# A two-layer macaron network in one kernel: norms, recurrence and routing laid between the units of the two expert mixtures

## What is computed

```
x = x + 0.5 * moe(layernorm(x))          # first mixture
x = x + rwkv(layernorm(x))               # recurrence over the tokens
x = x + 0.5 * moe(layernorm(x))          # second mixture, same weights
x = x + 0.5 * quant_ffn(layernorm(x))
x = x + attention(layernorm(x))          # 16 heads, softmax over all 2048 tokens
x = x + 0.5 * quant_ffn(layernorm(x))

moe(x):  logits = x @ router_w + router_b;  the two best of 8 experts, softmax over those two -> gates
         h = relu(x @ w1[e] + b1[e])     # 128 -> 512, for every expert e
         sum over e of gates[:, e] * (h @ w2[e] + b2[e])
rwkv(x): x_prev = x one token earlier;  k, v, r from three mixes of x and x_prev
         p' = max(p + w, k);  a' = exp(p+w-p')*a + exp(k-p')*v;  b' likewise without v
         out = (sigmoid(r) * (e1*a + e2*v)/(e1*b + e2)) @ Wo
layernorm(x) = (x - mean) / sqrt(var + eps), over the 128 channels, no gain and no bias
```

## Time and profile before

| what | value |
|---|---|
| median of 3 runs | 2174.58 us (2172.72 to 2175.76) |
| the profiled execution's own time | 2179.51 us |
| its span, first to last instruction | 2177.7 us |
| TensorE matmul busy | 2010.9 us, 92% |
| VectorE busy | 1852.0 us, 85% |
| ScalarE busy | 1521.1 us, 70% |
| GpSimd busy | 1414.8 us, 65% |
| mean granted TensorE clock | 0.944 |

### The profile page before, as it was taken

How to read it: one execution, slowest core, us unless ns; L and a number is a source line. 1 busy time by engine, 2 the same in 40 slices (tenths; PEclk the granted TensorE clock), 3 DMA queues, 4 the chain that set the end, 5 groups by cost and what they waited for, 6 DMA issues and landing times. The chain is left out here.

```text
span 2177.7 us, 25650 instructions
## 1 busy us (share of the span) xinstructions
PE 2010.9 (92%) x8288; PEld 1438.4 (66%) x8288; DVE 1852.0 (85%) x2001; ACT 1521.1 (70%) x1873; POOL 1414.8 (65%) x660
## 2 busy tenths in 40 slices
PE   5999638999869999999999999999999999999877
PEld 4888427887546766766766676676766667666545
DVE  5888886887677999899899899989989989999885
ACT  4666435665417878788788787877878888788753
POOL 1000010000308999899989989989998998999872
PEclk6999758998779999999999999999999999999987
DMA  2210002110050303123031231312313122130000
GB/s 105 76 49 30 0 0 60 49 49 15 4 116 6 71 15 74 28 55 76 13 74 31 52 67 23 73 20 62 69 21 68 30 58 57 31 69 17 5 1 20
DMA packets 77272, 94.68 MB, mean 43 GB/s; under 512 B 31755, under 2 KB 35211, under 8 KB 76870
## 3 DMA queue, kind: packets, MB, share of 16 engines
q1 hardware_dynamic: 77142, 93.04, 18.8%
HBM read 41.11 MB, written 1.42 MB: 20 GB/s over the span
## 5 line engine op out<-in xcount | busy, mean ns | idle before, releaser
L490 POOL TENSOR_TENSOR p_l<-p_raw,p_h 128x1024 fp32r<-128x1024 f32 x512 | 1241.8, 2457 | 148.1 <-ACT p_h L1068 133.2
L1065 ACT ACTIVATE p_raw<-ps 128x1024 f32<-128x1024 f32 x512 | 567.2, 1108 | 241.7 <-PE ps L711 240.9
L1387 DVE TENSOR_REDUCE m_part<-ps 128x1 f32<-128x1024 f32 x480 | 584.9, 1218 | 125.7 <-PE ps L688 124.7
L1068 ACT ACTIVATE p_h<-ps 128x1024 fp32r<-128x1024 f32 x512 | 523.4, 1022 | 0.0
L710 PE MATMUL ps<-qa,ka 128*128 128x512 f32 x1024 | 445.8, 435 | 2.0 <-ACT m_t L1036 2.0
L711 PE MATMUL ps<-qb,kb 65*128 65x512 f32 x1024 | 409.2, 400 | 0.0
L725 PE MATMUL ps<-p_h,v_hl 128*128 128x512 f32 x1024 | 402.6, 393 | 1.1 <-POOL p_l L490 0.9
L1381 DVE TENSOR_REDUCE l_sum<-p_raw 128x128 f32<-128x1280 f32 x256 | 377.2, 1477 | 0.4
L688 PE MATMUL ps<-ka,qa 128*128 128x512 f32 x960 | 314.9, 409 | 12.6 <-DVE m_part L1387 12.4
L728 PE MATMUL ps<-p_l,v_hl 128*64 128x512 f32 x1024 | 321.3, 395 | 0.0
L1367 DVE TENSOR_REDUCE p_raw<-p_raw 128x128 f32<-128x1024 f32 x256 | 309.2, 1209 | 12.2 <-ACT p_raw L1065 12.2
(11 more groups left out here) (187 smaller groups left out, 2653.4 us busy)
## 6 DMA issues: line engine op xcount, KB each, us to landing
big<-g_scratch SPq DMA_DIRECT2D x64, 256.0 KB, 3.2
xnp<-r_scratch SPq DMA_DIRECT2D x59, 256.0 KB, 3.9
qa<-qk_hi SPq DMA_DIRECT2D x112, 128.0 KB, 2.3
ka<-qk_hi SPq DMA_DIRECT2D x56, 128.0 KB, 2.4
kb<-qk_hi SPq DMA_DIRECT2D x56, 128.0 KB, 2.4
ka<-xnp SPq DMA_DIRECT2D x28, 128.0 KB, 2.4
qb<-xnp SPq DMA_DIRECT2D x28, 128.0 KB, 2.4
ka<-qk_low SPq DMA_DIRECT2D x28, 128.0 KB, 3.7
```

The lines of the kernel that those rows point to most:

```text
L490: nc.gpsimd.tensor_tensor(p_l[:, g % 4, :, :], slots(g), p_h[:, g % 4, :, :].bitcast(fp32), ALU.subtract).then_inc(pl_done, 1)
L1065: af(slots(g), s_t, ACT.Exp).then_inc(raw_done, 1)
L1068: af(p_h[:, g % 4, :, :], s_t, ACT.Exp).then_inc(ph_done, 1)
L1387: nc.vector.tensor_reduce(m_part[:, it, half:half + 1], ps[:, 4:6, :].rearrange("p b n -> p (b n)"), AX.X, ALU.max).then_inc(s_max, 1)
```

## The change

**One loop.** The six steps up to `layer_norm(3)` are replaced by `mixtures()` on each engine: a loop over ticks. In tick t (0 to 255) TensorE makes the first product of unit t and the second product of unit t - 4. Norm, routing, recurrence and weight preparation are cut into chunks of 512 tokens (weights: one expert), and each of their operations has a tick, by constants written by hand. 16 ticks precede the first unit.

**Bias in a weight row.** After a norm the 128 channels of a token sum to zero, so x[127] = -(sum of the others) and x @ w = sum over c < 127 of x[c] * (w[c] - w[127]). Row 127 of x becomes a row of ones, and row 127 of w1 becomes b1. The eviction then needs no bias: ScalarE writes relu straight into `h_h` (fp32r), and VectorE makes the low part from PSUM, max(ps, 0) - h_h. For this SP also loads w1's last row, repeated over 127 partitions, and VectorE subtracts it.

**Other moves.** The low parts of x and of w1 and the adding of an expert to x go from VectorE to GpSimd (0.5 goes into the gates' eviction); the recurrence's products with v, e1 and r are on GpSimd. `layer_norm(3)` waits for all expert additions at once. Layer 1 is the same but for the numbers that it waits for.

The core of the diff:

```diff
+TICKS = 2 * NC * UNITS
+HEAD_START = 16
+ROUTE_AT = (-16, 0, 20, 59, 95, 131, 167, 187)
+RWKV_AT = (40, 76, 112, 148)
+WEIGHTS_AT = (-8, -5, 2, 6, 10, 14, 18, 22)
+WEIGHT_PARTS = ((0, 1), (1, 2), (2, 4), (4, 8))
+N_MEAN, N_CEN, N_SQR, N_VAR, N_STD, N_REC, N_SPREAD, N_OUT = 0, 1, 1, 4, 5, 6, 8, 9
+R_HIGH, R_LOGITS, R_LOW, R_TOP, R_SECOND, R_EXP, R_GATES, R_TURN, R_ROWS = 10, 11, 11, 12, 13, 14, 15, 18, 19
+K_EXP = (18, 19, 20, 21)
+W_BASE, W_HI, W_LO, W2_HI, W2_LO = 0, 1, 1, 2, 3
...
 SP:
-            sp.dma_start(w1_raw, a["w1T"]).then_inc(w1_loaded, 16)
-            sp.dma_start(w2_raw, a["w2T"]).then_inc(w2_loaded, 16)
+            def load_weights(i):
+                lo, hi = WEIGHT_PARTS[i]
+                sp.dma_start(w1_raw[0:C - 1, lo:hi, :], a["w1T"][0:C - 1, lo:hi, :]).then_inc(w1_loaded[i], 16)
+                sp.dma_start(w1_base[0:C - 1, lo:hi, :],
+                             a["w1T"][C - 1:C, lo:hi, :].to_broadcast([C - 1, hi - lo, H0])).then_inc(w1_loaded[i], 16)
+                sp.dma_start(w2_raw[:, lo:hi, :, :], a["w2T"][:, lo:hi, :, :]).then_inc(w2_loaded[i], 16)
+            load_x(0)
+            sp.dma_start(b1[:, :], a["b1T"].rearrange("p e a -> p (e a)")).then_inc(b1_loaded, 16)
+            sp.wait_ge(const_row, 1)
+            sp.dma_start(x_h[C - 1:C, :].bitcast(fp32), h_l[0:1, :, :].rearrange("p a n -> p (a n)").bitcast(fp32)).then_inc(row_loaded, 16)
+            load_weights(0)
...
+            load_weights(1)
+            load_x(1)
+            load_weights(2)
+            for c in range(2, NC):
+                load_x(c)
+            load_weights(3)
+            sp.wait_ge(b1_done, 1)
+            sp.dma_start(w1_raw[C - 1:C, :, :].rearrange("p e n -> p (e n)"), b1_row[:, :]).then_inc(b1_moved, 16)
...
 TensorE:
+            def first_product(t):
+                j, u = t // UNITS, t % UNITS
+                e, ht = u // HT0, u % HT0
...
+                if u == 0:
+                    pe.wait_ge(xl_done, j + 1)
+                if j == 0 and ht == 0:
+                    pe.wait_ge(w_lo, e + 1)
+                if t >= 4:
+                    pe.wait_ge(h_done, t - 3)
...
+                for t in range(-HEAD_START, TICKS + TAIL):
+                    if 0 <= t < TICKS:
+                        first_product(t)
+                    if 0 <= t - LAG < TICKS:
+                        second_product(t - LAG)
+                    route(t)
+                    rwkv(t)
...
 ScalarE:
+            def high_weights(t):
+                for e, base in enumerate(WEIGHTS_AT):
+                    if t - base == W_HI:
+                        act.wait_ge(w1_ready, e + 1)
+                        act.wait_ge(b1_moved, 16)
+                        af(w1_h[:, e, :], w1_raw[:, e, :], ACT.Copy).then_inc(w_hi, 1)
...
+            def high_hidden(t):
+                act.wait_ge(h_ps, t + 1)
+                if t >= 4:
+                    act.wait_ge(w2_done, t - 3)
+                af(h_h[:, t % 4, :], ps[:, t % 4, :], ACT.Relu).then_inc(h_hi, 1)
...
 VectorE:
+            def base_weights(t):
+                for e, base in enumerate(WEIGHTS_AT):
+                    if t - base == W_BASE:
+                        dve.wait_ge(w1_loaded[[e < hi for _, hi in WEIGHT_PARTS].index(True)], 32)
+                        tt(w1_raw[0:C - 1, e, :], w1_raw[0:C - 1, e, :], w1_base[0:C - 1, e, :], ALU.subtract).then_inc(w1_ready, 1)
...
+            def low_hidden(t):
+
+                dve.wait_ge(h_hi, t + 1)
+                stt(h_l[:, t % 4, :], ps[:, t % 4, :], 0.0, h_h[:, t % 4, :].bitcast(fp32), ALU.max, ALU.subtract).then_inc(h_done, 1)
...
+            def mixtures():
+                dve.wait_ge(const_ready, CONST)
+                for t in range(-HEAD_START, TICKS + TAIL):
+                    if 0 <= t < TICKS:
+                        low_hidden(t)
+                    n = (t - LAG - HT0) // HT0
+                    if t % HT0 == 0 and 0 <= n < 2 * E * NC:
+                        gate_expert(n)
+                    base_weights(t)
+                    route(t)
+                    rwkv(t)
...
 GpSimd:
+            def low_weights(t):
+                for e, base in enumerate(WEIGHTS_AT):
+                    if t - base == W_LO:
+                        pool.wait_ge(w_hi, e + 1)
+                        nc.gpsimd.tensor_tensor(w1_l[:, e, :], w1_raw[:, e, :], w1_h[:, e, :].bitcast(fp32), ALU.subtract).then_inc(w_lo, 1)
...
+            def add_expert(n):
+
+                cols = chunk(n // E % NC)
+                pool.wait_ge(y_gate, n + 1)
+                if n % E > 0:
+                    pool.wait_ge(y_add, n)
+                nc.gpsimd.tensor_tensor(x[:, cols], x[:, cols], y_gated[:, n % 2, :], ALU.add).then_inc(y_add, 1)
```

More of the change, by code:

```diff
@@ L105, in macaron_kernel @@
         rank = sb("rank", [128, E], where=one)
[L106 to L114, removed]
+        lg = sb("lg", [128, TPC, E], where=one)
+        lg2 = sb("lg2", [128, TPC, E], where=one)
+        eq = sb("eq", [128, TPC, E], where=one)
+        best = sb("best", [128, TPC, E], where=one)
+        second = sb("second", [128, TPC, E], where=one)
+        gates = sb("gates", [128, TPC, E], where=one)
+        rt = sb("rt", [128, 8, TPC], where=one)
         rwkv_w = sb("rwkv_w", [C, 4, C], where=one)
@@ L117, in macaron_kernel @@
         decay = sb("decay", [C, 2], where=one)
+        xw = sb("xw", [C, CH + 1], where=one)
+        k_sum = sb("k_sum", [C, CH + 1], where=one)
+        b_sum = sb("b_sum", [C, CH + 1], where=one)
+        a_sum = sb("a_sum", [C, CH + 1], where=one)
         one.close()
[L119 to L126, removed]
+        raw_flat = w1_raw[:, :, :].rearrange("p e n -> p (e n)")
+        base_flat = w1_base[:, :, :].rearrange("p e n -> p (e n)")
+        w_diff, w_k, w_v, w_r, w_fv, w_ev, w_num, w_den = [raw_flat[:, i * CH:i * CH + CH] for i in range(8)]
+        w_mix = [base_flat[:, i * CH:i * CH + CH] for i in range(3)]
+        w_f1, w_f2, w_e1, w_e2, w_inv = [base_flat[:, (3 + i) * CH:(4 + i) * CH] for i in range(5)]
         two = ExitStack()
-        wgu = sb("wgu", [C, 2, H1], fp32r, two)
-        wd = sb("wd", [128, HT1, C], fp32r, two)
         ka = [sb(f"ka{i}", [128, T], fp32r, two) for i in range(2)]
@@ L179, in macaron_kernel @@
         small_loaded = sem("small_loaded")
[L180 removed]
+        w1_loaded = [sem(f"w1_loaded{i}") for i in range(len(WEIGHT_PARTS))]
+        w2_loaded = [sem(f"w2_loaded{i}") for i in range(len(WEIGHT_PARTS))]
+        b1_loaded, b1_ps, b1_done, b1_moved = sem("b1_loaded"), sem("b1_ps"), sem("b1_done"), sem("b1_moved")
+        rwkv_loaded, row_loaded, const_row = sem("rwkv_loaded"), sem("row_loaded"), sem("const_row")
         l1_loaded = sem("l1_loaded")
@@ new lines, in route @@
+            def route(t):
+                for j, base in enumerate(ROUTE_AT):
+                    at, k, c = t - base, 2 * (j // NC), j % NC
+                    norm(k, c, at)
+                    if at == R_LOGITS:
+                        pe.wait_ge(small_loaded, 16 * 3)
+                        pe.wait_ge(ln_out, norm_index(k, c) + 1)
+                        for i in range(TPC):
+                            tile = slice(c * CH + i * 128, c * CH + i * 128 + 128)
+                            last = mm(ps[:, 7, E * (i + 1):E * (i + 2)], xn[:, tile], rw[:, :], start=True, stop=True)
+                        last.then_inc(rt_logits, 1)
+                    elif at == R_TURN:
+                        pe.wait_ge(rt_gates, j + 1)
+                        outs = sum(b + K_PROJECT_OUT < t for b in RWKV_AT)
+                        if outs > 0:
+                            pe.wait_ge(rwkv_added, outs)
+                        for i in range(TPC):
+                            last = mm(ps[0:E, 7, i * 128:i * 128 + 128], gates[:, i, :], ident[:, :], start=True, stop=True)
+                        last.then_inc(gt_ps, 1)
@@ new lines, in rwkv @@
+            def rwkv(t):
+                for c, base in enumerate(RWKV_AT):
+                    at = t - base
+                    norm(1, c, at)
+                    if at in K_PROJECT:
+                        j = K_PROJECT.index(at)
+                        if c == 0 and j == 0:
+                            pe.wait_ge(rwkv_loaded, 32)
+                        pe.wait_ge(mixed, 3 * c + j + 1)
+                        if j == 2:
+                            pe.wait_ge(kvr_done, 3 * c + 1)
+                        mm(ps[:, 7 if j == 1 else 6, :], rwkv_w[:, j, :], w_mix[j], start=True, stop=True).then_inc(kvr_ps, 1)
+                    elif at == K_PROJECT_OUT:
+                        pe.wait_ge(wkv_out, c + 1)
+                        pe.wait_ge(rt_read, sum(b + R_LOGITS < t for b in ROUTE_AT))
+                        mm(ps[:, 7, :], rwkv_w[:, 3, :], w_num, start=True, stop=True).then_inc(o_ps, 1)
```

571 lines of the change are left out of this document (304 added, 267 removed).

## The result

2286.19 us (median of 4 runs) against 2175.17: ratio 1.0505, 95% interval 1.0482 to 1.0529. The change makes the kernel 111 us slower. The profiled execution took 2287.96 us against 2179.51, and its last expert addition ends at 635.24 us instead of 525.94: the 109 us between these two executions all lie ahead of that point.

A forecast was written before the change was run, and what follows sets the result against it. TensorE was taken to bound the mixtures, a VectorE and ScalarE chain the gap. 199 (head) + 2 + 409 (loop) + 10 (stalls) + 4 = 624 us against 526, +98, taken as +92: 2267 us median, range 2236 to 2325.

The forecast's parts named there:

- Direction and mechanism: Slower: the first product waits for b1_moved, issued behind all weight loads, whose 127-row DMAs use one engine; 0.83 for slower.
- The head, 199 us: Time until the first product of the first mixture, forecast at about 199 us instead of 50.40.
- one engine's time for 4.16 MB: Loading raw w1 and the repeated row as 127-row DMAs on a single DMA engine: 179 us.
- my lower bound: Same loads with everything at 25.5 GB/s: 163 us in place of 179; the upper bound was 219.
- My allowance of 6 us for "alone": Taking +92 instead of +98 us, since a DMA engine alone should do a little better than among 16.
- The 5 us behind b1_moved: Two weight copies, x's high part and three GpSimd differences between b1_moved and the first product: 5 us.
- The loop, 409 + 2 + 10 + 4 = 425 us: First product to last expert addition: TensorE's work 409, clock rise 2, stalls 10, closing chain 4 us.
- The stall term: Loop time lost when other engines hold up TensorE: 10 us taken, bounds 0 and 40.
- rival 2: VectorE bounds the recurrence's ticks through in-order waits with ScalarE and GpSimd: 40 to 60 us of stalls, 2310 us; chance 0.10.
- counted as covered: ScalarE's loop work, 177 plus some 100 us including table loads, was taken to be hidden behind TensorE.
- The gap: Between the two mixtures, 119 us before the change, almost all forecast to go; that was the gain.
- Rival 1: The 127-row loads spread over all 16 engines: first product at 31 us, 2105 us in all; chance 0.16.

The follow-up runs named there:

- experiment 1: Changed kernel with w1 rows and repeated row loaded over 128 rows, b1's row moved after all w1 loads: 2140.06 us, 0.9836 of the kernel before.
- experiment 2: Changed kernel with only the repeated-row loads over 128 rows, w1 rows still at 127: 2213.25 us (one run).
- experiment 3: Changed kernel with each 127-row load cut into 126 rows and 1 row: 2150.88 us (one run).
- experiment 4: Changed kernel, 127-row loads kept, b1's row moved right behind the first expert's loads: 2268.2 us (one run).
- experiment 9: Kernel before the change, its one 128-row w1 load cut into 127 rows and 1 row: 2243.94 us, ratio 1.0302.
- experiment 6: Version with 112 + 15 rows and b1's row early, the loop's Sqrt, Ln and Sigmoid made Copy (no table loads): 2116.37 us.
- experiment 7: Version with 112 + 15 rows and b1's row early, GpSimd's five recurrence products covering 64 of 512 columns: 2111.80 us.
- experiment 8: Version with 112 + 15 rows and b1's row early, with both no table loads and narrow GpSimd products: 2103.74 us.
- experiment 10: Experiment 8 with VectorE's recurrence operations also at 64 of 512 columns, except the last addition to x: 2098.34 us.

## Why the prediction was right, and where its terms were off

- **Direction and mechanism** were right: the first product waits for b1_moved, that waits for the load queue, and the queue is slow because 127 rows run on one engine. Experiments 1 to 3 show the engine count, 4 that the wait on b1's move is not the cause by itself, and 9 the cost of a 127-row load without the new loop. The rule of the Trainium skill, "DMA: Bandwidth & Descriptors", section "Why a DMA increments its semaphore by 16 and not by 1", that 127 partitions go to one engine, is now borne out by the packet counts (over eight loads 121 end packets fewer than with 128 rows, where 120 were due).
- **The head, 199 us; measured 179.9.** The term that was off is one engine's time for 4.16 MB: I had 179 us from packets timed while sixteen engines were at work. b1's row had landed by 175.3, and 4.16 MB at the 25.6 GB/s of the lone engine make 163, my lower bound: alone, a 2 KB packet took 0.080 us, not 0.094 or, for the repeated row, 0.108. My allowance of 6 us for "alone" had the right sign and a third of the size. The 5 us behind b1_moved were 4.6.
- **The loop, 409 + 2 + 10 + 4 = 425 us; measured 455.** The stall term was mis-sized: I took 10 us, with 0 to 40 as bounds, and 26 us came off when three causes were taken out (experiments 6 to 8, 10): table loads 10, hold-ups beside GpSimd 9, VectorE's own queue 7. So the mechanism of rival 2, in-order waits between VectorE, ScalarE and GpSimd, is real, at about half the price that I had given it. Part of it are table loads in ScalarE's queue, which I had counted as covered. I knew of the hold-up from the earlier trace rows and named it, but gave it no price of its own. My averages couldn't show this: VectorE, which I had put at 355 us, was busy for 338 us of the loop. With all three gone the loop still took 430 us from the first product to the edge, against 415 without stalls. Of these 15 us some 5 are in the inserted matmuls, whose groups are busy for 66 us there and not 61; TensorE is idle for 11.5 us in all, the edge included. The granted clock after the idle head (0.66 in 190 to 195 us of the kernel after, nearer to the lower level of 1.2 GHz than to the full one) and short chain waits of the norms have a part too; how they share the rest wasn't tried.
- **The gap** went as forecast, 119 us less and about 60 us of inserted matmuls more.
- The two misses, 19 us too much in the head and 30 us too little in the loop, partly cancel: +98 in the sum, +92 taken, +109 measured in the profiled executions and +111 in the medians. That the time came out within 19 us of the forecast, and inside the range, is in part luck.
- **Rival 1** (even spreading, 2105 us) named what experiment 1 brings about; the loop, 30 us longer than its terms, makes it 2140 and not 2105, and with b1's row early it is 2127.

## What to carry to other kernels

Before cutting one row or one partition off a tile to free it for something else, divide the row count: 128 is 16 x 8, 127 is prime, and in these runs the load went to a single DMA engine, with the shares of later DMAs queued behind it. Cut as 112 + 15, or load the full 128 and overwrite. When work is laid into another engine's shadow by averages, list what runs beside it on the shared resources: a VectorE planned at 87%, and busy for 74% of the loop, still went with 26 us of stalls, by hold-ups beside GpSimd, table loads between relus and its own queue.

## What was unexpected of the hardware

- The sixteenth share that a well-spread DMA has on the busy engine delays all of it: w2's last part landed 67.6 us after its issue began.
- SP itself was held up while it issued behind the slow loads: single issues took 27 and 39 us, where others take 0.4, and the second is the greater part of those 67.6 us. In order of time, SP's queue of the kernel after:

```profile
80.30 27.09 SPq L341 DMA_DIRECT2D w_base<-in_w1T  x1
107.43 38.99 SPq L343 DMA_DIRECT2D w_raw<-in_w2T  x1
146.47 3.03 SPq L360 DMA_DIRECT2D w_raw<-b_row  x1
```

- One engine alone moved 2 KB packets at 25.6 GB/s (0.080 us each), as fast as 16 KB packets in company (25.5).
